# k in the second staging bank, reordered heads, and pads and weight loads moved in a two-layer gated Flamingo block

## The reference

```python
x = x + tanh(g_xattn[0]) * attention0(layernorm(x), ctx)      # 16 heads of 16, strict causal mask
x = x + tanh(g_ffn[0])   * moe0(layernorm(x))                 # 8 experts, F = 256, top 2, and a shared expert
x = x + tanh(g_xattn[1]) * attention1(layernorm(x), ctx, len) # 16 heads, keys up to a length
x = x + tanh(g_ffn[1])   * moe1(layernorm(x))                 # 8 experts, F = 1024, top 2, cosine gate
```

## Time and profile before

| | |
|---|---|
| median of 3 runs | 1718.82 us (1715.0 to 1719.96) |
| the profiled execution | 1725.34 us |
| its span, first to last instruction | 1723.3 us |
| TensorE busy | 1376.0 us (80%) |
| VectorE busy | 1075.0 us (62%) |
| ScalarE busy | 797.8 us (46%) |
| GpSimd busy | 732.2 us (42%) |
| mean granted TensorE clock | 0.930 of 2.4 GHz |

### The profile page before, as it was taken

How to read it: one execution, slowest core, us unless ns; L and a number is a source line. 1 busy time by engine, 2 the same in 40 slices (tenths; PEclk the granted TensorE clock), 3 DMA queues, 4 the chain that set the end, 5 groups by cost and what they waited for, 6 DMA issues and landing times. The chain is left out here.

```text
span 1723.3 us, 39989 instructions
## 1 busy us (share of the span) xinstructions
PE 1376.0 (80%) x12001; PEld 1174.9 (68%) x12002; DVE 1075.0 (62%) x3573; ACT 797.8 (46%) x1760; POOL 732.2 (42%) x694
## 2 busy tenths in 40 slices
PE   3798889888872777735888888888727999999997
PEld 3577777767651766734565566565417999999997
DVE  4587768786753455433788787877645555555543
ACT  2364545554430555531555455555513454444543
POOL 4334444443231566644335454543233334545522
PEclk9999999999985999965999999999968999999999
DMA  2434333433217577642333333332263423434422
GB/s 89 108 97 122 85 108 101 126 79 97 57 56 226 104 130 116 108 89 69 100 101 102 109 95 110 100 105 73 68 178 106 99 48 87 97 86 98 95 40 43
DMA packets 213628, 168.25 MB, mean 98 GB/s; under 512 B 21462, under 2 KB 207096, under 8 KB 213240
## 3 DMA queue, kind: packets, MB, share of 16 engines
q1 hardware_dynamic: 181112, 126.05, 26.6%
q0 software_dynamic: 26880, 35.80, 12.1%
q10 hardware_dynamic: 5504, 4.75, 1.0%
HBM read 63.80 MB, written 51.56 MB: 67 GB/s over the span
## 5 line engine op out<-in xcount | busy, mean ns | idle before, releaser
L1811 POOL DMA_INDIRECT out_rows<-e_y,e_token x68 | 110.3, 1622 | 235.7 <-DVE e_y L1867 215.9
L1893 ACT ACTIVATE e_h<-e_h,t_up_bias 128x256 f32<-128x256 f32 x272 | 110.6, 444 | 209.1 <-PE e_h L1929 209.1
L773 POOL DMA_INDIRECT routed_rows_dram<-r_rows,r_slot x128 | 127.3, 995 | 187.3 <-DVE r_rows L1043 104.7
L941 DVE TENSOR_REDUCE a_row_max<-a_scores 128x2 f32<-128x512 f32 x256 | 171.6, 680 | 48.7 <-PE a_scores L1584 48.5
L1272 ACT ACTIVATE s_w_rows<-a_scores_t 128x384 f32<-128x384 f32 (+1 forms) x256 | 134.8, 547 | 107.2 <-PE a_scores_t L1602 64.1
L1272 ACT ACTIVATE a_probs<-a_scores_t 128x384 f32<-128x384 f32 (+1 forms) x256 | 135.9, 544 | 100.1 <-PE a_scores_t L1602 51.1
L1944 PE MATMUL e_y_bank<-e_down_hi,e_hidden_hi 128*128 128x256 f32 x544 | 157.8, 290 | 3.1 <-DVE e_hidden_lo L1840 3.1
L1929 PE MATMUL e_h<-e_xs_hi,e_up_hi 128*128 128x256 f32 x544 | 154.8, 285 | 3.7 <-DVE e_xs_lo L1832 3.5
L2102 POOL DMA_INDIRECT x_mid_dram<-l_y,l_token x76 | 119.8, 1577 | 83.8 <-ACT l_token L2196 46.1
L1929 PE MATMUL e_h<-e_xs_lo,e_up_hi 128*128 128x256 f32 x544 | 154.0, 283 | 0.0
L1944 PE MATMUL e_y_bank<-s_k_stack,e_hidden_hi 128*128 128x256 f32 x544 | 153.8, 283 | 0.0
(11 more groups left out here) (287 smaller groups left out, 4326.8 us busy)
## 6 DMA issues: line engine op xcount, KB each, us to landing
s_q_stack<-a_parts SPq DMA_DIRECT2D x384, 64.0 KB
s_k_stack<-a_parts SPq DMA_DIRECT2D x384, 64.0 KB
l_xs_rows<-routed_rows_dram SPq DMA_DIRECT2D x42, 258.0 KB
e_xs_rows<-routed_rows_dram SPq DMA_DIRECT2D x36, 258.0 KB
a_ctx_rows<-in_ctx SPq DMA_DIRECT2D x32, 256.0 KB, 3.2
t_up<-in_L_ffn_W SPq DMA_DIRECT2D x8, 1024.0 KB
t_down<-in_L_ffn_W SPq DMA_DIRECT2D x8, 1024.0 KB
routed_rows_dram<-pad_rows ACTq DMA_DIRECT2D x16, 258.0 KB, 10.0
```

The source lines that it names most:

```text
L773: pool.indirect_dma_start(out=xs, out_offset=bass.IndirectOffsetOnAxis(ap=slot[p][:, k, c:c + 1], axis=0), in_=rows[p][:, k, c, :], in_off ...
L941: nc.vector.reduce_max(row_max[:, :, h], bank[:].rearrange("p (c t) -> p c t", c=TC), AX_X).then_inc(maxed, 1)
L1811: pool.indirect_dma_start(out=x_acc, out_offset=bass.IndirectOffsetOnAxis(ap=token[p][:, c:c + 1], axis=0), in_=y[p][:, c, :], in_offset=N ...
L1893: nc.scalar.activation(out, h_bank[g][:, at:at + TS], act_func, bias=routed.up_bias[:, bass.ds(e * FC + fc, 1)]).then_inc(hidden_ready, 1)
```

## The change

k goes to bank 1 directly behind q and the mixing, so it no longer waits for `q_ready`; the second half of the maxima goes to bank 0 behind it and waits for q there. The heads of the jobs change: in layer 0 V from 11 to 13 and the context from 13 to 14; in layer 1 V from 11 to 12, the rank from 9 to 8 and the mark from 8 to 6. `turn_route` moves from 13 to 14, `shared_down` from 15 to 6 with `bend_hidden` from 12 to 4 and `add_shared` from the step's end to head 7. Each `need` names the new last reader.

In the last two steps the shared expert's jobs, the pads and the table get places of their own: pads start from both the SP and the ACT queue (`pad_regions`, four each) once `next_row` is final, and the table stands around the shared expert's last jobs. The weight loads, the spare tiles (now in layer 0 alone) and the rows behind x are started in step 3 instead of after the pipeline. In layer 1 five fills of 258 KB are thus gone.

```diff
-        GATE_AT, O_AT, V_AT, RANK_AT, CTX_AT = (1 if soft else 2, 4, 11, 9, 13)
-        MARK_AT = 5 if soft else 8
+        GATE_AT, O_AT, V_AT, RANK_AT, CTX_AT = (1, 4, 13, 9, 14) if soft else (2, 4, 12, 8, 13)
+        MARK_AT = 5 if soft else 6
+        DOWN_AT = 6
+        LOAD_AT = 3
...
+        def pad_regions(eng, first):
+            eng.wait_ge(pads_placed, 1)
+            for e in range(first, E, 2):
+                row = eng.value_load(routed.pad_start[0:1, e:e + 1], min_val=0, max_val=E * R - TS)
+                eng.dma_start(xs[bass.ds(row, TS), :].rearrange("(c p) w -> p c w", p=P), pad_rows[:]).then_inc(pads_sent, 16)
...
+            spares = SPARE_TILES if causal else 0
+            def pad_ends():
+                sp.wait_ge(r_consts_ready, 1)
+                for n in range(spares):
+                    at = E * R + n * TS
+                    sp.dma_start(xs[at:at + TS, :].rearrange("(c p) w -> p c w", p=P), pad_rows[:]).then_inc(x_stored, 16)
+                sp.dma_start(x_acc[tokens:tokens + TS, :].rearrange("(c p) d -> p c d", p=P), pad_rows[:, :, 0:D]).then_inc(x_stored, 16)
...
+                if i.at(0) == LOAD_AT:
+                    load_experts(sp)
+                    pad_ends()
+                if i.at(-2) == B - 1:
+                    pad_regions(sp, 0)
                 if i.has(-2 if soft else -1):
                     store_x(i)
             pipeline(sp, step, B, FIRST, LAST, HEAD, TAIL)
-            load_experts(sp)
-            sp.wait_ge(r_consts_ready, 1)
-            for n in range(SPARE_TILES):
...
@@ VectorE: k, and the order of a step
-                nc.vector.tensor_tensor(qk[:, KC:2 * KC, :], stage[0][:].rearrange("p (c s) -> p c s", c=KC),
+                nc.vector.tensor_tensor(qk[:, KC:2 * KC, :], stage[1][:].rearrange("p (c s) -> p c s", c=KC),
...
+            def place_pads():
+                dve.wait_ge(counted, B)
+                nc.vector.tensor_copy(routed.pad_start[:], next_row[:]).then_inc(pads_placed, 1)
...
+                    if h == DOWN_AT - 2 and soft and i.has(-2) and i.has(-1):
+                        bend_hidden(i)
+                    if h == DOWN_AT + 1 and soft and i.has(-2) and i.has(0):
+                        add_shared(i)
+                    if h == 10 and i.at(-2) == B - 1:
+                        place_pads()
+                    if h == 11 and soft and i.has(-2) and i.has(-1) and not i.has(0):
+                        add_shared(i)
-                    if h == 12 and soft and i.has(-2):
-                        bend_hidden(i)
+                    if h == 14 and i.at(-2) == B - 1:
+                        table_of_tiles()
+                        if soft:
+                            bend_hidden(i)
+                        rows_of_tiles()
+                        if soft:
+                            add_shared(i)
-                if soft and i.has(-2):
-                    add_shared(i)
@@ ScalarE
                 if i.has(2):
                     evac_q(i)
+                if causal and i.has(2):
+                    evac_k(i)
                 if i.has(0):
                     stack_max(i, 0, 1)
-                if causal and i.has(2):
-                    evac_k(i)
...
-                    if h == 3 and soft and i.has(-2):
+                    if h == (3 if i.has(-1) else 14) and soft and i.has(-2):
                         bend_up(i)
-                    if h == 13 and i.has(1):
+                    if h == 12 and i.has(1):
                         stack_max(i, 1, 0)
+                    if h == 11 and i.at(-2) == B - 1:
+                        act.wait_ge(r_consts_ready, 1)
+                        pad_regions(act, 1)
-                    if h == 13 and i.has(-1):
+                    if h == 14 and i.has(-1):
                         evac_route(i)
@@ TensorE
             def project_k(i):
                 b, p = i.at(2), i.par(2)
                 pe.wait_ge(ctx_t_ready, b + 1)
-                pe.wait_ge(q_ready, b + 1)
-                project_t(stage[0], 1, ctx_t[p], k_done)
+                project_t(stage[1], 1, ctx_t[p], k_done)
...
             def turn_ctx(i):
                 p = i.par(3)
                 pe.wait_ge(ctx_loaded[p], (i.half(3) + 1) * 16)
-                need(pe, counted, i.upto(-2))
-                need(pe, v_ready, i.upto(1))
-                need(pe, x_updated, i.at(0))
+                if i.has(1):
+                    need(pe, v_ready, i.upto(1))
+                elif i.has(2):
+                    need(pe, k_ready, i.upto(2))
...
+                if i.has(2):
+                    project_k(i)
                 if i.has(0):
                     turn_max_late(i)
-                if i.has(2):
-                    project_k(i)
...
-                    if h == 2 and soft and i.has(-2):
+                    if h == (2 if i.has(-1) else 10) and soft and i.has(-2):
                         shared_up(i)
-                    if h == V_AT and i.has(1):
-                        project_v(i)
+                    if h == DOWN_AT and soft and i.has(-2) and i.has(0):
+                        shared_down(i)
                     if h == RANK_AT and i.has(-2):
                         rank(i)
+                    if h == 10 and soft and i.has(-2) and not i.has(0):
+                        shared_down(i)
+                    if h == V_AT and i.has(1):
+                        project_v(i)
                     if h == CTX_AT and i.has(3):
                         turn_ctx(i)
-                    if h == 13 and i.has(-1):
+                    if h == 14 and i.has(-1):
                         turn_route(i)
-                    if h == 15 and soft and i.has(-2):
-                        shared_down(i)
```

More of the change, by code:

```diff
@@ L1076, in add_shared, with tail_step, table_of_tiles @@
                                                in1=at, op0=ALU.mult, op1=ALU.add).then_inc(sh_added, 1)
+            steps = [0]
+            def tail_step(ins):
+                steps[0] += 1
+                ins.then_inc(table_step, 1)
+                dve.wait_ge(table_step, steps[0])
+            def place_pads():
+                dve.wait_ge(counted, B)
+                nc.vector.tensor_copy(routed.pad_start[:], next_row[:]).then_inc(pads_placed, 1)
+            def table_of_tiles():
+                tail_step(nc.vector.tensor_tensor(count[:], next_row[:], region_start[:], ALU.subtract))
+                tail_step(nc.vector.tensor_tensor(beyond[:], count[:].unsqueeze(2).to_broadcast((P, E, J)),
+                                                  full_steps[:].unsqueeze(1).to_broadcast((P, E, J)), ALU.is_gt))
+                tail_step(nc.vector.reduce_sum(n_tiles[:], beyond[:], AX_X))
+                tail_step(nc.vector.tensor_copy(ends[:, 0:1], n_tiles[:, 0:1]))
+                for e in range(1, E):
+                    tail_step(nc.vector.tensor_tensor(ends[:, e:e + 1], ends[:, e - 1:e], n_tiles[:, e:e + 1], ALU.add))
+                nc.vector.tensor_copy(routed.used_tiles[:], ends[:, E - 1:E])
+                tail_step(nc.vector.tensor_tensor(past[:], tile_iota[:].unsqueeze(2).to_broadcast((P, tiles, E)),
+                                                  ends[:].unsqueeze(1).to_broadcast((P, tiles, E)), ALU.is_ge))
+                tail_step(nc.vector.reduce_sum(region[:], past[:], AX_X))
@@ L1160, in _ @@
-            tail_step(nc.vector.reduce_sum(n_tiles[:], beyond[:], AX_X))
-            tail_step(nc.vector.tensor_copy(ends[:, 0:1], n_tiles[:, 0:1]))
-            for e in range(1, E):
-                tail_step(nc.vector.tensor_tensor(ends[:, e:e + 1], ends[:, e - 1:e], n_tiles[:, e:e + 1], ALU.add))
-            nc.vector.tensor_copy(routed.used_tiles[:], ends[:, E - 1:E])
-            tail_step(nc.vector.tensor_tensor(past[:], tile_iota[:].unsqueeze(2).to_broadcast((P, tiles, E)),
-                                              ends[:].unsqueeze(1).to_broadcast((P, tiles, E)), ALU.is_ge))
@@ L1249, in stack_max @@
                 turned = max_t[half][p]
-                nc.scalar.activation(turned[:], stage[half][0:MP * HH, 0:S // 2].bitcast(BF16), ACT.Copy).then_inc(max_t_ready, 1)
+                nc.scalar.activation(turned[:], stage[0][0:MP * HH, 0:S // 2].bitcast(BF16), ACT.Copy).then_inc(max_t_ready, 1)
                 act.wait_ge(max_t_ready, 2 * b + half + 1)
@@ L1449, in turn_max @@
                 wait_apart(pe, max_ready, 2 * i.at(d) + half + 1, consts_ready, N_READY)
-                turned = stage[half][0:MP * HH, 0:S // 2].bitcast(BF16)
+                turned = stage[0][0:MP * HH, 0:S // 2].bitcast(BF16)
                 for c in range(TC):
@@ L1481, in gate_rows_of @@
                 need(pe, r_xn_t_ready, b + 1)
-                need(pe, max_t_ready, 2 * i.upto(0))
-                if soft:
+                if i.has(2):
+                    need(pe, k_ready, i.upto(2))
+                elif i.has(0):
+                    need(pe, v_ready, i.upto(0))
+                elif soft and not i.has(-1):
```

(21 more changed lines are left out.)

107 lines of the change are left out of this document (52 added, 55 removed).

## The result

The changed kernel takes 1723.43 us (median of 14 runs, 1715.41 to 1730.79), the kernel before 1716.28 (14 runs, 1707.16 to 1721.64) on the same chips. The ratio is 1.0047, 95% interval 1.0027 to 1.0068: slower by half a per cent, where 1643 us was forecast and 1605 to 1695 given as the range. The profiled execution of the changed kernel has a span of 1720.8 us, close to its median; that of before lay 9 us above its median, so the two traces are compared stage by stage and not by their spans.

What follows compares the result with a forecast made beforehand. TensorE's order of work, with waits on two shared staging banks, was taken as the bound. 24 + 27 + 18 + 2 + 4 + 3 - 2 = 76 us off 1725.34 gave 1649, 1643 us for the median; range 1605 to 1695.

Steps and rivals of the forecast that it cites:

- The six rows: TensorE's waits in eleven steady steps of layer 0's attention, adding to 41.1 us, nearly all its unfilled time.
- The new wait that was seen: Layer 0's steady steps: turn_ctx at head 14 waits for V to leave bank 1, priced at 1.2 us a step.
- 2.2 us a step: Layer 0's steady steps: 3.7 us of waits removed less 1.5 of new ones, 24 us over eleven steps.
- The clock: TensorE's clock, below full rate for some 25 us of layer 1's stretch: shorter gaps gain 3 us, ends -3 and 10.
- Layer 1: Layer 1's steady attention steps: 2.5 us saved a step, 27 us over eleven, ends 0 and 54.
- The tails: Ends of the attention phases: layer 0's 18 us shorter (ends 13 and 23), layer 1's 2 us (ends 0 and 5).
- the last gate: Layer 0's tail: with shared_down of batch 14 ahead of turn_route, the gate waits for r_xn_t alone, 5.2 us earlier.
- the two chains: Layer 0's tail ends with row transfers, next phase at 528.6 us, or with the shared expert's store and barrier, 527.5.
- The loads: Weights, spares and pad issued in step 3: hidden at DMA share 0.84, costing 2 us for both layers, ends 0 and 8.
- the rule on issuing engines: Pads on two queues share sixteen DMA engines, so the split saves only issue time, at most 5.8 us.
- Only the tails pay: Rival: VectorE is the bound behind the banks' waits, so the steps gain little; about 1690 us, chance 0.15.
- The slower rival: Delay during GpSimd's transfers falls on evac_v, turn_ctx waits up to 4 us more a step; from 3.4 slower, chance 0.07.

Runs made afterwards that it cites:

- tails_only: Kernel before with only the changed kernel's last two steps, two-queue pads, table and loads in step 3, old step order otherwise: 1697.53 us, ratio 0.9896.
- turn10: Changed kernel with VectorE's transpose of pv (turn_heads) in layer 0 at head 10 instead of 11: 1723.29 us, ratio 1.0027 to the kernel before.
- v12: Changed kernel with V in layer 0 at head 12 instead of 13, ahead of mixing group 2: 1715.76 us, ratio 0.9997 to the kernel before.
- after_send0: Changed kernel, V still at 13, with GpSimd's row transfers a few us into the next step in layer 0 alone: ratio 1.0174 to the kernel before.
- v12_send0: Changed kernel with V at head 12 and GpSimd's row transfers a few us into the next step, both in layer 0 alone: 1690.55 us, ratio 0.9869.
- load_late: Changed kernel with weight loads, spares and x pad started behind the pipeline again: 1741.85 us, ratio 1.0145 to the kernel before.
- new1: Changed kernel's attention phase in layer 1; in layer 0 the old step order with the new tails and loads: 1669.41 us, ratio 0.9892 to the kernel before.
- v12_gate2: Changed kernel with V at head 12 and the gate at head 2 instead of 1, both in layer 0: 1692.67 us, ratio 1.0066 to the kernel before.

## Why the prediction was wrong

**The reading of the bound failed.** The prediction said that TensorE's order of work sets these steps, since the waits of the earlier trace rows fill nearly all of its idle time, and took each removed wait as time saved, less the new waits that it saw. The six rows were true and their sum was no gain. While TensorE stood at V or at k, VectorE and ScalarE went on with their own lists; with these waits gone TensorE waited for the two engines elsewhere. Even the steps at full clock show it: 28.1 us each in the changed kernel, of which TensorE waits 3.4, and 27.8 in the mean of nine in `tails_only`, with 3.5 of idle time. The new wait that was seen, turn_ctx at 1.2 us, was priced right (1.16). What was missing is the mixing behind `turn_heads`, 1.85 us a step. It comes from moving V from head 11 to behind head 13's mixing; `turn10` and `v12` each take it away, by VectorE's order and by V's place. With shared_down's two VectorE operations moved up to heads 4 and 7 as well, VectorE is late just there; that part was not tried by itself.

**Taking that wait away gives little**, because others lie close behind: k leaving bank 1 ahead of the gate, then `next_row`, the exponentials, update_x. Forecast for layer 0 was 2.2 us a step. Over eleven steps the idle time of TensorE fell by 0.46 a step. Taking the mixing's wait away gained 9 us in `v12` and some 3 in `turn10`, of the 26 that the new order costs.

**The clock had the wrong sign.** The prediction took 3 us of gain. In layer 0's stretch the granted clock went from 0.99 to 0.95, and TensorE needed 12.7 us more for the same matmuls. Against `tails_only`, whose stretch is 10.0 us shorter, it is 13.9 us more of busy time less 3.9 of idle time. Most of this is the clock: six of the eleven steps fell below full clock, and they are 11.0 us longer than six of 28.1, while in `tails_only` two steps did. Some 5 us aren't: at full clock too TensorE is busy for 24.7 us in a step and for 24.1 to 24.4 in the old order. In stretches of the kernel after:

```profile
134.00:138.60 4.60, 2.75 (x36) 1.86 (x36) 4.43 (x26) 1.97 (x5) 2.12 (x3) 1.00 0.44 103
138.60:142.00 3.40, 2.76 (x17) 2.34 (x15) 2.04 (x13) 0.60 (x2) 0.98 (x1) 0.50 0.13 32
...
353.80:381.90 28.10, 24.70 (x268) 20.19 (x267) 20.86 (x113) 14.83 (x34) 12.81 (x14) 1.00 0.40 105
```

The first holds a mixing wait of 1.85 us, and right behind it the clock is at 1.2 GHz; the last is a whole step with the same wait in which it stayed at 2.4. The Trainium skill ("TensorE: Matmul & The Clock Gate", "Part 1: The HAM clock gate (the "warmup" mystery)") has the clock set by how busy the engine has been, and the rows agree in kind. Across kernels the longest waits of layer 0 and the clock go together at the ends: 4.5 us and 0.92 in `after_send0`, 0.9 (and a single one of 1.9) and 1.00 in `v12_send0`. In between they don't: `tails_only` has waits of up to 2.0 us at 0.99. That the waits are to blame, and not something else in the new order, was only argued. Steps at full clock take 28.1 us in the new order and 26.9 to 28.9 in the old one.

**Layer 1.** Forecast 27 us, of which the stretch shows 4.9, and against `tails_only` it is a loss (308.5 to 305.6). The rank's wait was to go with the mark two heads earlier; it grew from 0.63 to 1.26 us a step. The prediction moved the mark by its place in VectorE's list and took the length of its operations as given. At its new place one of them takes 0.9 us more, because it meets GpSimd's `a_parts`; over eleven steps that is 10 us more of VectorE's time ahead of the rank. The exponentials' wait grew from 0.3 to 1.5 us a step on the 1715 chips, and to 0.6 on the 1685 chips.

**The tails were right, in part by luck.** Forecast 18 for layer 0's tail, 2 for layer 1's, less 2 for the loads in the steps, 18 in all; `tails_only` gained 1.04% or 18 us (10 to 26). From head 0 of the last step with scores its layer 0 tail took 78.0 us, 19.9 less than before, and layer 1's 79.6, 1.9 less. Inside layer 0's tail one step was off: the last gate was to come 5.2 us earlier for being behind r_xn_t alone. It came 1.1 earlier from the last scores, since shared_down of batch 14 waits for `next_row` and still stands ahead of turn_route. Rank to next phase was 20.7 us, forecast 20.8, but by the other of the two chains. The sum took the row transfers (11.2 us from their end to the next phase). They ended at 533.02, 12.5 us ahead of it; what ended last was the shared expert, its store issued at 541.11 and the next phase 4.4 us later, where the prediction had 19.7 for this chain. So the agreement to 0.1 us is chance. From 530 to 538 us the DMA engines' share was 1.06 with two queues issuing pads and 1.06 in the kernel before, and they moved 273 and 345 GB/s: there is no sign that the second queue adds to what they move. This agrees with the rule on issuing engines; the split alone was not tried.

**The loads were right:** DMA share 0.87 in the step that carries them, forecast 0.84, and no score waited on a stack transfer in the stretch. `load_late` shows that moving them back costs 17 us.

**The rivals.** "Only the tails pay" had a mechanism of the right kind, another engine behind the banks' waits, with a chance of 0.15 and a floor at zero gain for the steps. It named VectorE alone; k's evacuation and the exponentials are ScalarE's. What it missed is that the steps can lose: the new order cost 26 us, of which the order around head 13 accounts for some 9 (`v12`). The slower rival named the delay during GpSimd's transfers and put it on evac_v. Turn_ctx waited no more than 1.2 us, so not there; in `v12` the same delay fell on evac_k. What makes up the rest of the 26 us is not shown; the traces have it mostly as a lower clock in layer 0 and as the longer waits of layer 1.

## What to carry to other kernels

A list of one engine's waits says where it stands, not what it would gain. Before a job is moved, look at what the other engines do during its time: if one of them is catching up there, the wait will turn up at the next hand-over to it. Here the cheapest warning was VectorE's order between heads 9 and 13, read against the mixing's bank. Look as well at what runs beside a moved operation: the same 128x32 operation took 0.19 us at one head and 1.10 at another.

Test an edit of many parts in its parts. The half of this change that only touches the tails and the loads is 1.0% faster by itself; the other half took it back and more. Layer 0's steps came well below the old ones only where V stood ahead of the mixing and the row transfers were elsewhere; either alone, or the transfers' move in the old order, gave nothing or cost. A ratio taken on one kind of chip need not hold on another when the edit moves waits that one of them has.

## What was not expected of the hardware

Around the end of a batch's row transfers by GpSimd, ScalarE and VectorE can take up TensorE's results some 2 us late: evac_k in `v12` started at 346.98 for a bank filled at 344.97. The size differs with the chip. With the old order of layer 0 k waited 10.6 us in eleven steps of `tails_only` on one chip and not once in `new1` on another. What in the chip holds them is open; the runs show only that moving the transfers moves the waits.

A small VectorE operation that runs beside GpSimd's `a_parts` (128x512, two of 1.1 us) can take six times as long: `r_one_hot` 1.10 us and not 0.18 to 0.19, in all eleven steps of layer 1 of the kernel after and of layer 0 of `v12_gate2`. In the kernel before it never stood there; beside GpSimd's `a_mask_row` it took 0.19 and beside nothing 0.18. Not every small operation is held: `a_max_parts` (128x16) took 0.18 to 0.19 beside the same `a_parts` in three steps of the kernel before. Which operations are, the runs don't show.

The kernel before took 1684 and 1686 us on two chips and 1715 to 1718 on others, 2% apart and four times the effect measured here. In the traces of the changed order this lies in attention and not in the experts: layer 1's attention took 465 us in `new1` and 482 in the kernel after, its experts 435.5 and 433.9.
